# Four-layer graph network on one core: in the third layer GpSimd begins the gathers of a step only when ScalarE has copied the turned tiles of the step two places back

## The reference

```python
def _L2_gnn_ref(x, edge_idx, edge_weights, W_att1, b_att1, W_att2, b_att2, W_lin, b_lin, W_ih, b_ih, W_hh, b_hh):
    src, dst = edge_idx
    lin_x = x @ W_lin.T + b_lin
    feat = jnp.concatenate([x[src], edge_weights, x[dst]], axis=1)      # 64 + 16 + 64
    h = jax.nn.relu(feat @ W_att1.T + b_att1)                           # 144 wide, per edge
    scores = (h @ W_att2.T + b_att2)[:, 0]
    e = jnp.exp(scores - segment_max(scores, src)[src])
    alpha = e / segment_sum(e, src)[src]
    msg = segment_sum(alpha[:, None] * lin_x[dst], src)
    ...                                                                 # a gated update of the nodes
x = _layernorm(x + _L0(...)); x = _layernorm(x + _L1(...))
x = _layernorm(x + _L2(...)); x = _layernorm(x + _L3(...))
```

## Time and profile before

| | us |
|---|---|
| median of 3 runs | 14,022.34 (13,997.5 to 14,025.02) |
| the profiled execution | 13,975.26, its span 13,973.5 |
| the third layer's steps, from the first gather to the last copy of a turned tile | 8,332.6 to 11,173.2 of the span |

### The profile page before, as it was taken

The page is one execution under the profiler, slowest core; times in us unless marked ns, Lnnn a source line. Parts: engine busy times, 40 slices in busy tenths (PEclk is TensorE's granted clock), DMA queues, the critical chain, the costliest instruction groups (busy, mean ns, idle before and its releaser), DMA issues. The chain is left out here.

```text
span 13973.5 us, 56497 instructions
## 1 busy us (share of the span) xinstructions
PE 2437.7 (17%) x11588; PEld 1897.7 (14%) x11588; DVE 5735.1 (41%) x14196; ACT 2306.2 (17%) x3572; POOL 8899.8 (64%) x8546
## 2 busy tenths in 40 slices
PE   0122332341000000000000004444444451000000
PEld 0122222230000000000000003333333330000000
DVE  8778676875222222311111114544455533222223
ACT  0122333320111111122221201111111111111111
POOL 0267766662777777677777765555555446777776
PEclk8555555555555555555555557777777755555555
DMA  4000000011211111111111112222222201111111
GB/s 164 17 13 13 12 10 11 11 28 21 51 49 48 49 49 49 45 50 47 47 46 47 47 41 55 62 59 62 60 62 61 60 17 44 49 49 47 49 49 46
DMA packets 688745, 628.08 MB, mean 45 GB/s; under 512 B 453486, under 2 KB 511495, under 8 KB 687505
## 3 DMA queue, kind: packets, MB, share of 16 engines
q0 software_dynamic: 273056, 240.52, 9.6%
q1 hardware_dynamic: 413614, 372.84, 8.2%
q10 hardware_dynamic: 1728, 11.11, 0.2%
HBM read 319.01 MB, written 304.83 MB: 45 GB/s over the span
## 5 line engine op out<-in xcount | busy, mean ns | idle before, releaser
L1102 POOL DMA_INDIRECT l_rows<-table,l_sources x4704 | 4942.1, 1051 | 1612.4 <-issue 1569.6
L1102 POOL DMA_INDIRECT l_pair<-table,l_slab x1568 | 1499.3, 956 | 1315.0 <-DMA l_pair<-seeds 831.7
L548 POOL DMA_INDIRECT e_rows<-in_rec,base x1568 | 1770.3, 1129 | 784.5 <-issue 464.2
L1299 DVE TENSOR_TENSOR_SCAN l_totals<-l_factor,banks 128x510 f32<-128x510 f32 (+3 forms) x672 | 752.7, 1162 | 1899.0 <-ACT banks L1454 1898.1
L1230 DVE TENSOR_TENSOR l_score<-l_rows,base 128x14 f32<-128x14 f32 x224 | 43.0, 192 | 3215.0 <-DMA l_rows<-table,l_sources 3215.0
L1464 ACT COPY l_kept<-l_totals 128x476 f32<-128x476 f32 (+3 forms) x672 | 638.8, 967 | 3715.0 <-issue 2920.4
L1416 PE MATMUL banks<-ident,l_kept 128*65 128x128 f32 (+2 forms) x4 | 1.9, 464 | 6743.7 <-DVE junk L1348 4565.8
L1416 PEld LDWEIGHTS banks<-ident,l_kept 128*65 128x65 f32 (+2 forms) x4 | 0.7, 170 | 6745.0 <-DVE junk L1348 4566.4
L703 PE MATMUL banks<-Z 125*128 125x98 bf16 x3200 | 622.2, 366 | 1656.1 <-DVE Z L686 1479.7
L1406 PE MATMUL banks<-w_each,l_turned 128*128 128x288 f32 (+1 forms) x1344 | 660.6, 580 | 1384.4 <-ACT l_turned L1486 1026.2
L407 ACT COPY area<-area 128x2048 f32<-128x2048 f32 x342 | 642.5, 1926 | 1484.3 <-DVE area L332 1277.1
(11 more groups left out here) (323 smaller groups left out, 5630.0 us busy)
## 6 DMA issues: line engine op xcount, KB each, us to landing
l_rows<-table,l_sources POOLq DMA_INDIRECT x4704
sums<-l_kept SPq DMA_DIRECT2D x112, 476.0 KB
sums<-l_kept SPq DMA_DIRECT2D x224, 231.0 KB
sums<-l_kept SPq DMA_DIRECT2D x112, 462.0 KB
seeds<-zeros SPq DMA_DIRECT2D x130, 392.0 KB
sums<-l_kept SPq DMA_DIRECT2D x112, 448.0 KB
l_pair<-seeds SPq DMA_DIRECT2D x224, 224.0 KB
e_rows<-in_rec,base POOLq DMA_INDIRECT x1568
```

The costliest lines, as they stand in the source:

```text
L548: GP.indirect_dma_start(e_rows[:, u, g, :], None, A["rec16"], bass.IndirectOffsetOnAxis(e_ids[:, s * G16 + g:s * G16 + g + 1], 0)).then_in ...
L1102: GP.indirect_dma_start(pair[:, u, g, 0:D] if gated else rows[:, u, g, :], None, table[l], bass.IndirectOffsetOnAxis(at, 0)).then_inc(rows ...
L1299: V.tensor_tensor_scan(flat(totals[:, s % 2, h, 0:n, :]), flat(factor[:, s % 2, 0:n, :]), flat(fresh[s % 2][h][:, 0:n, :]), 0.0, ALU.mult, ...
```

## The change

One wait is added in front of the gathers of each step of the third layer, from the third step on: GpSimd begins them only when both copies of step `s - 2` (`turned`) are done. Nothing else changes; no instruction is added, removed or moved, and no other layer is touched (`gated` is true in the third alone).

```diff
                         if gated:
                             pool.wait_ge(*slab_in[u].done(r))
+                            if s >= 2:
+                                pool.wait_ge(*done("turned", s - 2))
 
                         for g in range(G):
```

## The result

The changed kernel takes 13,678.7 us (median of 4 runs, 13,662.9 to 13,683.8), the kernel before 14,018.0 (4 runs, 13,997.5 to 14,025.0): a ratio of 0.9755, 95% interval 0.974 to 0.977. The profiled execution took 13,683.1 us with a span of 13,681.3. The forecast was 13,895 with a range down to 13,770: the sign came out and the size did not; how much of the mechanism held is told behind the experiments.

The account below looks back on a forecast made before the run. Runs of gathers were taken to nearly stop TensorE in the third layer. A 26 us start plus 222 steps at 12.1 us gave 2,712 instead of 2,840.6 us, 129 less: 14,022 to about 13,895, range 13,770 to 14,120.

Parts of the forecast that it names:

- What bounds the kernel: Third layer: TensorE nearly stops some 5 us into a run of gathers; "remote" idle time before the dots is 760.7 us.
- Take turns: Third layer: work on TensorE and runs of gathers alternate, inferred from coincidence in time; a step's seven gathers take 8.8 us.
- The gate instead of the load: GpSimd's pauses, 831.7 us in 95, would end at ScalarE's copy instead of the near rows' load.
- The start: Third layer's beginning: step 1's copy ends about 26 us after the first gather instead of 84.
- It starts again about 2 us after the run: Third layer: TensorE recovers about 2 us after a run of gathers ends.
- The steps: Third layer after the start: 222 steps at 12.1 us, 2,686 us together.
- A run of two steps: Third layer: fourteen gathers, then a pause of 7.0 us, 24.2 us for two steps, 12.1 us a step.
- A run of one step: Third layer: 8.8 us of gathers plus about 4.6 us for recovery, transposes and copy, 13.4 us a step.
- The mixture: Third layer: runs of 14 gathers expected; half the groups in each form, 12.75 us a step, would be no change.
- one step at a time: Rival, third layer: every run is one step at 13.4 us, 14,182 us in all; chance 0.22 including mixtures near it.
- much faster: Rival, third layer: pauses shrink to 4.0 us throughout, 10.6 us a step, 13,560 us in all; chance 0.09.
- TensorE is slow for its own reasons: Rival, third layer: gathers only coincide with slowness, the gate frees nothing and costs 30 us, 14,022 to 14,052; chance 0.17.

Follow-up runs that it names:

- held-up jobs: Four jobs, nothing changed in the kernel before, which takes 13,969 to 14,023 us there (medians).
- rest: Kernel before, no gate, plus one unused 128x2048 iota on GpSimd after each third-layer step's seven gathers: ratio 0.977.
- rest2x: Kernel before, no gate, plus two unused 128x512 iotas per third-layer step, after gathers 2 and 6: 10.10 us a step.
- gate3: Changed kernel with the wait on the copy three steps back instead of two; ratio 1.0001 to the kernel before, which took 11,942 us there.
- free job: One of two jobs, nothing changed in the kernel before, which takes 11,942 and 11,945 us there.
- gate1_b: Changed kernel with the wait on the copy one step back instead of two, where the kernel before takes about 14,000 us: 13.45 us a step.
- gate1: Changed kernel with the wait on the copy one step back instead of two, where the kernel before takes 11,942 us: 13.46 us a step.
- half_b: Kernel before, no gate, third-layer gathers fetching rows for partitions 0 to 63 only, the other half zero: ratio 0.998.
- split43: Changed kernel plus a second wait before each step's last three gathers, on the hidden layer two steps back: 0.967 and 1.000 in the two kinds of job.
- after_again: The changed kernel unchanged, run again beside the kernel before in another job: ratio 0.9754 (0.971 to 0.979).
- rest2s: Kernel before, no gate, plus two unused 128x64 iotas (0.22 us) per third-layer step; the job's three iota kernels cost 0.8 to 3.1%.

## Why the prediction was right in sign and wrong in size

**What bounds the kernel: right in the held-up jobs.** Long rows of gathers do hold up what waits for TensorE, as the earlier trace rows suggested: GpSimd's added iotas (rest) end it without touching anything else. "Take turns" was too strong, since with rows of three and four gathers both go on side by side (rest2x). What I did not see, and the trace of one execution couldn't show, is that in some jobs there is nothing of the kind. The Trainium skill's rule ("SBUF — State Buffer", section "Who interferes with whom": PE and ACT never wait on anyone) agrees with gate3 in the free job, whose dots have 467.4 us of waits for TensorE by name and none "remote". In the held-up jobs what TensorE makes came late while GpSimd gathered (48 dots waited over 7 us in the trace of before, and an added iota ended it). Whether TensorE itself waited there, which would be against the rule, no run shows.

**The gate instead of the load: right.** 140 waits end with the copy, and none with the near rows' load. The loads are off the path.

**The start, predicted 26 us to step 1's copy, was 37.8** (8,355.9 to 8,393.7). I had the run end after two steps. But the copy of step 0 is made at 8,368.5, before the second step's gathers are out, so a third step follows. Copies and GpSimd at that place:

```profile
8367.87 0.59 ACT L1488 COPY l_turned<-banks 128x512 f32<-128x512 f32 x1 [0.27 <-issue]
8392.65 1.07 ACT L1488 COPY l_turned<-banks 128x512 f32<-128x512 f32 x2 [24.10 <-remote]
```

```profile
8380.86 0.94 POOL L1104 DMA_INDIRECT l_pair<-table,l_slab  x1 [0.30 <-issue]
8394.48 0.94 POOL L1104 DMA_INDIRECT l_pair<-table,l_slab  x1 [12.67 <-ACT l_turned L1488]
```

46 us saved instead of 58. "It starts again about 2 us after the run" is also too simple: after these 21 gathers the copy came 10.8 us after the last one.

**The steps, predicted 12.1 us, took 11.23: this is the step of the prediction that failed.** It was to give 70 us and gave 264. Its two prices were too high, and its mixture of runs was wrong as well.

- *A run of two steps* was put at 12.1 us a step and took 11.1 (65 runs, each from its first gather to the next run's). I took the 7.0 us of the earlier trace rows as its pause, though the row said that a load ended it and though I had read there that the copy was done 4.0 us after the last gather. Measured, the pause is 4.4 us on average. The pair that I had read was not typical either: in the trace of before the 49 pauses after two steps are 5.6 us on average and such a step takes 11.6 us. One pair is no average.
- *A run of one step* was put at 13.4 us, from 2 us of recovery, two transposes and a copy, all behind the last gather, and took 11.4 (90 runs), with a pause of 2.9 us. With the gate of **one** step such a step does take 13.45 us (gate1_b), but the free job has 13.46 (gate1), so that no recovery is in it. In gate1 the pause of 4.9 us is the gathers' landing (TensorE begins to transpose 1.6 us after the last gather, by the median), the transposes and the copies (a step's last gather starts at 9,009.3, its transposes at 9,011.7, the next step's gathers at 9,015.1). With the gate of two steps the tiles to be turned have landed a run earlier, so the landing at least is out of the pause; how the rest of the 2 us saved is made up was not taken apart.
- *The mixture.* I expected pairs, and 90 of the 156 runs were single steps. With the forecast's own prices this mixture would be 12.6 us a step and no gain at all. That the sign came out is therefore luck in part: both prices were too high by enough to make up for it.

Both forms being near the 11.23 measured, it didn't matter which occurred, and the "one step at a time" rival (0.22) and "much faster" (0.09) described one outcome between them: many runs of one step, and fast.

**The rivals.** "TensorE is slow for its own reasons" falls with gate1_b and rest. "One step at a time" came (90 of 156 runs) without its price. "Nothing outside the layer changes" held to 18 us.

**What is not shown.** Whether TensorE itself stands still or only its signals come late; the rows of both would look alike, since its records are the hand-over. Whether it is GpSimd's issuing that does it or the transfers that it has set off: an iota breaks both rows, and half_b speaks only against their size. Why some jobs do this and others do not. No run here takes the gathers away with everything else kept.

## What to carry to other kernels

If a wait is moved from one releaser to another, price the new pause by the time at which the new releaser was ready in the trace, not by the pause that stands there. If engines stand idle while another one issues one kind of instruction without a break, put something between those instructions before you shorten anything: here useless work made the kernel faster, and a wait on a stage two steps back does the same at no cost where it isn't needed (split43: 0.967 in the held-up job, 1.000 in the free one). Run the kernel before in every job, on several chips and more than once on the same: here gates and cuts were worth 2.4 to 3.9% in some jobs and nothing in others, and a time from another job could not have been compared. Do not take the price of a pause from one example when the trace has 49.

## What the hardware showed that I had not expected

- The same kernel takes 11,942 and 11,945 us in two jobs and about 14,000 in the others, and chip number 2 is in both kinds. Only part of this is the third layer (1,989 us with gate3, 2,841 in the trace of before). The other three layers, which no kernel here changes, tell the kinds apart too: the first of their 4,704 gathers (`l_rows`) starts at 3,072.6 us in gate3 and at 3,500.7 in the trace of before, and their mean is 947 and 1,051 ns, with a median of 947 in both. In gate3 4 of them take over 1.5 us, in before 377. The two jobs with chip number 2 differ in the same way: in after_again 348 take over 1.5 us and the first starts at 3,527.9, in rest2s it is 4 and 3,070.7.
- The pause does not simply grow with the run: on the changed kernel it is 2.9 us on average after 7 gathers and 4.4 after 14. After the one run of 21, at the layer's start, it is 12.7, but the four runs of 21 in after_again have 5.8 on average.
- What breaks a row of gathers may itself be work: in a held-up job 0.73 us of iota after every three or four gathers, 1.5 us a step of added work, took the step from 12.42 to 10.10 us.
